# Second layer's ReLU joined with VectorE's weighting, and the scores' two spread products made one

## What is computed

```python
# graph attention, per graph
Wh = h @ W;  f_i = Wh @ a1;  f_j = Wh @ a2
e = leaky_relu(f_i[:, :, None] + f_j[:, None, :], 0.2)
e = where(adj > 0, e, NEG_INF)
out = elu(softmax(e) @ Wh)

# first mixture, per token; top_i, routing_weights from the router
h1 = relu(features @ expert_w1 + expert_b1)
h2 = relu(h1 @ expert_w2 + expert_b2)
expert_out = h2 @ expert_w3 + expert_b3
combined = sum(take(expert_out, top_i) * routing_weights)
```

## Time and profile before

| | before |
|---|---|
| median of 3 runs | 577.62 us (577.44 to 578.25) |
| profiled execution | 582.93 us |
| its span, first to last instruction | 580.9 us |
| PE busy | 544.8 us (94%) |
| DVE busy | 453.2 us (78%) |
| ACT busy | 420.9 us (72%) |
| POOL busy | 229.0 us (39%) |

### The profile page before, as it was taken

How to read it: one execution, slowest core, us unless ns; L and a number is a source line. 1 busy time by engine, 2 the same in 40 slices (tenths; PEclk the granted TensorE clock), 3 DMA queues, 4 the chain that set the end, 5 groups by cost and what they waited for, 6 DMA issues and landing times.

```text
span 580.9 us, 14943 instructions
## 1 busy us (share of the span) xinstructions
PE 544.8 (94%) x3713; PEld 450.9 (78%) x3745; DVE 453.2 (78%) x1679; ACT 420.9 (72%) x1113; POOL 229.0 (39%) x442
## 2 busy tenths in 40 slices
PE   7789899999999999999999999999977999999993
PEld 6556677778787777878777787767756999999993
DVE  3776879889898898988989888776567187777777
ACT  1356577878878788787887878877653578888883
POOL 5212214442344424344243342431322046666665
PEclk9999999999999999999999999999997599999997
DMA  7604405043150422504225051131220567777732
GB/s 162 163 29 136 138 28 164 23 143 107 59 163 6 157 94 70 163 1 163 72 91 162 2 163 52 60 110 30 81 74 3 172 206 241 236 219 219 224 117 72
DMA packets 79135, 66.45 MB, mean 114 GB/s; under 512 B 10218, under 2 KB 64762, under 8 KB 79098
## 3 DMA queue, kind: packets, MB, share of 16 engines
q1 hardware_dynamic: 67914, 61.39, 34.9%
q10 hardware_dynamic: 11184, 4.63, 2.9%
HBM read 61.58 MB, written 4.42 MB: 114 GB/s over the span
## 4 chain that ended last, share of the span: by engine, by line
PE 72%; DVE 9%; issue 7%; ACT 5%; POOL 2%; DMA 2%; ACTq 0%; DVEq 0%; SPq 0%; POOLq 0%
PE bank L1593 12%; PE bank L1580 11%; PE bank L1893 5%; PE wide L206 5%; PE wide L1893 5%; PE bank L1903 5%; PE wide L1903 4%; PE bank L1572 3%; PE bank L1574 2%; PE wide L239 2%; PE bank L1573 2%; PE wide L231 2%; PE wide L199 2%; ACT h L851 2%; PE bank L1546 2%
## 5 line engine op out<-in xcount | busy, mean ns | idle before, releaser
L1593 PE MATMUL bank<-w,h2w 128*128 128x128 f32 x768 | 104.4, 279 | 6.5 <-DVE h2w L1147 6.5
L1593 PEld LDWEIGHTS bank<-w,h2w 128*128 128x128 f32 x768 | 94.8, 192 | 12.6 <-DVE h2w L1147 10.0
L1580 PE MATMUL bank<-h,w 128*128 128x512 f32 x192 | 100.1, 603 | 1.0 <-ACT h L851 1.0
L846 ACT ACTIVATE h<-bank,b 128x512 f32<-128x512 f32 x96 | 66.2, 689 | 37.9 <-PE bank L1580 37.7
L851 ACT ACTIVATE h<-bank,b 128x512 f32<-128x512 f32 x96 | 66.3, 691 | 13.2 <-PE bank L1574 12.7
L1147 DVE TENSOR_TENSOR h2w<-h,wide_w 128x512 f32<-128x512 f32 x96 | 64.9, 676 | 9.4 <-ACT h L846 8.5
L1572 PE MATMUL bank<-xnTh,w1h 128*128 128x512 f32 x96 | 61.9, 645 | 0.0
L100 POOL TENSOR_TENSOR route_var_eps<-route_mean_var,eps 128x4 f32<-128x4 f32 x17 | 11.2, 660 | 115.6 <-DVE route_mean_var L93 115.6
L100 POOL TENSOR_TENSOR at_var_eps<-at_mean_var,eps 128x4 f32<-128x4 f32 x32 | 12.2, 381 | 95.9 <-DVE at_mean_var L93 95.9
L268 ACT ACTIVATE at_pr<-at_lk,at_nm 128x128 f32<-128x128 f32 x124 | 39.9, 412 | 2.4 <-DVE at_nm L303 1.7
L1574 PE MATMUL bank<-xnTl,w1h 128*128 128x512 f32 x96 | 38.0, 396 | 0.0
(11 more groups left out here) (312 smaller groups left out, 1373.3 us busy)
## 6 DMA issues: line engine op xcount, KB each, us to landing
wide_w<-w_scratch SPq DMA_DIRECT2D x96, 256.0 KB, 4.7
mask<-in_L_ffn_W SPq DMA_DIRECT2D x124, 128.0 KB, 2.4
x<-in_x SPq DMA_DIRECT2D x16, 256.0 KB, 5.6
adj_in<-in_adj SPq DMA_DIRECT2D x16, 256.0 KB, 6.2
wide_w<-bmix_scratch SPq DMA_DIRECT2D x16, 256.0 KB, 3.6
xin<-in_x SPq DMA_DIRECT2D x15, 256.0 KB, 6.0
out<-at_pr ACTq DMA_DIRECT2D x8, 256.0 KB, 3.0
out<-at_prT ACTq DMA_DIRECT2D x7, 256.0 KB, 2.8
```

The costliest lines, as they stand in the source:

```text
L846: a.activation(h2[:, e % 2, :], b_h2[:, :], ACT.Relu, bias=b2[:, e:e + 1]).then_inc(h2_ready, 1)
L1580: pe.matmul(b_h2[:, :], w2[:, e, :], h1[:, e % 2, :], start=True, stop=True).then_inc(l2_done, 1)
L1593: last = pe.matmul(b_out[:, s], h2w[:, e % 2, s], w3[:, e, :], start=False, stop=(e == E0 - 1), skip_group_check=True)
```

## The change

**Experts.** `relu2` is gone from ACT. `weigh` reads layer 2's PSUM bank itself and takes max(z, -b2) times the weight. What this lacks against relu(z + b2), the weight times b2, is put into the third bias: POOL lays b2 out (`second_bias`), PE multiplies it by w3 in six products, DVE adds that to b3 (`merge_biases`), all once, before the experts start. `layer2` now waits for the `weigh` before it, and expert 1 of each round uses the bank `b_pool`. `weigh` 3, 4 and 5 stand earlier in DVE's list, and `route_exp` earlier in ACT's.

**Scores.** The order of `src` changes, so that each graph's six rows lie in partitions of their own (32 to a graph). ACT forms `rows` with a scale and a bias from SBUF columns (`inhalf`, `three`), and in four more instructions of 32 partitions the diagonal blocks of a new tile `blocks`; PE makes one product of the two instead of `spread`'s five.

```diff
+def form_rows(st, a, turned, inhalf, three):
+
+    a.activation(st["rows"][:, :], turned[:, :], ACT.Identity, bias=three[:, 1:2], scale=inhalf[:, 0:1])
+    for t in range(GG):
+        q = slice(t * P // GG, (t + 1) * P // GG)
+        last = a.activation(st["blocks"][q, t * P:(t + 1) * P], turned[q, :], ACT.Identity, bias=three[q, 0:1],
+                            scale=inhalf[q, 1:2])
+    last.then_inc(st["rows_ready"], 1)
+
-    a.activation(st["rows"][:, :], st["bank"].bitcast(BF16)[:, 0:P], ACT.Copy).then_inc(st["rows_ready"], 1)
+    form_rows(st, a, st["bank"].bitcast(BF16)[:, 0:P], inhalf, three)
...
     pe.matmul(st["bank"][:, :], identb[:, :], mask[:, cols(g)], start=True, stop=False, skip_group_check=True)
-    pe.matmul(st["bank"][:, :], st["rows"][:, :], spread[:, 0, :, :].rearrange("p t d -> p (t d)"), start=False,
-              stop=False, skip_group_check=True)
-    for t in range(GG):
-        last = pe.matmul(st["bank"][:, t * P:(t + 1) * P], spread[:, 1, t, :], st["rows"][:, :], start=False,
-                         stop=True, skip_group_check=True)
-    last.then_inc(st["z_done"], 1)
+    pe.matmul(st["bank"][:, :], st["rows"][:, :], st["blocks"][:, :], start=False, stop=True, skip_group_check=True)\
+        .then_inc(st["z_done"], 1)
...
-            def relu2(n, e):
-                a.wait_ge(l2_done, n + 1)
-                need(a, h2w_ready, n - 1)
-                a.activation(h2[:, e % 2, :], b_h2[:, :], ACT.Relu, bias=b2[:, e:e + 1]).then_inc(h2_ready, 1)
...
-                v.wait_ge(h2_ready, n + 1)
+                v.wait_ge(l2_done, n + 1)
                 v.wait_ge(w_loaded[e], 16 * g + 16)
                 need(v, l3_done, n - 1)
-                v.tensor_tensor(h2w[:, e % 2, :], h2[:, e % 2, :], wide_w[:, e, :], ALU.mult).then_inc(h2w_ready, 1)
+                v.scalar_tensor_tensor(h2w[:, e % 2, :], h2_bank(e), b2neg[:, e:e + 1], wide_w[:, e, :], ALU.max,
+                                       ALU.mult).then_inc(h2w_ready, 1)
...
                 pe.wait_ge(h1_ready, n + 1)
-                need(pe, h2_ready, n)
-                pe.matmul(b_h2[:, :], w2[:, e, :], h1[:, e % 2, :], start=True, stop=True).then_inc(l2_done, 1)
+                if e != 1:
+                    need(pe, h2w_ready, n - 1 if e == 2 else n)
+                pe.matmul(h2_bank(e), w2[:, e, :], h1[:, e % 2, :], start=True, stop=True).then_inc(l2_done, 1)
```

More of the change, by code:

```diff
@@ L154, in attn_stage @@
     st["rows"] = sb("rows", P, BF16)
+    st["blocks"] = sb("blocks", GW, BF16)
     st["lk"] = sb("lk")
@@ L400, in build @@
     centre = sb("centre", [P, P])
-    spread = sb("spread", [P, 2, GG, P], BF16)
+    inhalf = sb("inhalf", [P, 2])
+    three = sb("three", [P, 2])
+    halfmark = sb("halfmark", [P, 2, GG, 16])
+    threemark = sb("threemark", [P, 2, GG, 3])
+    unread = sb("unread", [P, 2 * P], BF16)
     zero = sb("zero", [P, GG, 2])
@@ L731, in _ @@
             p.memset(at1["src"][:, :], 0.0).then_inc(spread_step, 1)
[L732 to L738, removed]
+            p.memset(at0["blocks"][:, :], 0.0).then_inc(spread_step, 1)
+            p.memset(at1["blocks"][:, :], 0.0).then_inc(spread_step, 1)
+            p.memset(unread[:, :], 1.0).then_inc(spread_step, 1)
+            p.memset(halfmark[:, :, :, :], 0.0).then_inc(spread_step, 1)
+            p.memset(threemark[:, :, :, :], 0.0).then_inc(spread_step, 1)
+            p.wait_ge(spread_step, 7)
+            for mark, width in ((halfmark, 16), (threemark, 3)):
+                p.affine_select(out=mark[:, :, :, :], in_=mark[:, :, :, :], compare_op=ALU.not_equal, fill=1.0, base=0,
+                                pattern=[[-16, 2], [-32, GG], [-1, width]], channel_multiplier=1)\
+                    .then_inc(spread_step, 1)
             def later_constants():
@@ L874, in late_attention @@
                 a.wait_ge(at0["rows_done"], N + 1)
-                a.activation(at0["rows"][:, :], b_out.bitcast(BF16)[:, 0:P], ACT.Copy).then_inc(at0["rows_ready"], 1)
+                form_rows(at0, a, b_out.bitcast(BF16)[:, 0:P], inhalf, three)
                 for q in range(2):
@@ L971, in body @@
                     attn_act_prT(at0, a, i + 2)
-                if run and i0 > 0:
-                    relu2(n + 3, 3)
-                    relu1(n + 4, 4)
                 if route and i0 != -LEAD["route"]:
                     route_exp()
+                if run and i0 > 0:
+                    relu1(n + 4, 4)
                 if attn1:
-                    attn_act_rows(at1, a, i - 1)
+                    attn_act_rows(at1, a, inhalf, three, i - 1)
                 if route:
@@ L1347, in body @@
                     route_first(i + 1)
[L1348 to L1349 removed]
+                if run:
+                    weigh(n + 3, i, 3)
                 if route:
@@ L1355, in body @@
                     attn_dve_y(at0, v, i + 2)
-                if run and i0 > 0:
-                    weigh(n + 3, i, 3)
+                if run:
+                    weigh(n + 4, i, 4)
                 if route and i0 != -LEAD["route"]:
@@ L1659, in late_attention @@
                               start=True, stop=False, skip_group_check=True)
-                    pe.matmul(late_z[q], at0["rows"][:, :], spread[:, 0, 2 * q:2 * q + 2, :].rearrange("p t d -> p (t d)"),
-                              start=False, stop=False, skip_group_check=True)
-                    for t in range(2):
-                        last_t = pe.matmul(late_z[q][:, t * P:(t + 1) * P], spread[:, 1, 2 * q + t, :], at0["rows"][:, :],
-                                           start=False, stop=True, skip_group_check=True)
+                    last_t = pe.matmul(late_z[q], at0["rows"][:, :], at0["blocks"][:, lane[q]], start=False, stop=True,
+                                       skip_group_check=True)
                     last_t.then_inc(at0["z_done"], 1)
@@ L1732, in body @@
                     if i0 == -LEAD["attn0"]:
-                        pe.wait_ge(spread_step, 6)
-                    busy_fill(i0, 12 if i0 == -LEAD["attn0"] else 28)
+                        pe.wait_ge(spread_step, 9)
+                    busy_fill(i0, 12)
                     if i0 == -LEAD["route"]:
+                        pe.wait_ge(b2_step, E0 + 2)
+                        for e in range(E0):
+                            mixed_bias = pe.matmul(b_out[0:KB, 0:P], b2cols[:, e, 0:KB], w3[:, e, :], start=(e == 0),
+                                                   stop=(e == E0 - 1))
+                        mixed_bias.then_inc(b2_step, 1)
+                        busy(b_pool, 6)
                         route_transpose(i, i0)
@@ L1751, in body @@
                     pe.wait_ge(mask_ready, i + 3)
-                    attn_pe_scores(at0, pe, identb, mask, spread, i + 2)
+                    attn_pe_scores(at0, pe, identb, mask, i + 2)
                 if run and i0 > 0:
@@ L1806, in body @@
                 if attn1:
-                    attn_pe_scores(at1, pe, identb, mask, spread, i - 1)
+                    attn_pe_scores(at1, pe, identb, mask, i - 1)
                 if run:
```

75 lines of the change are left out of this document (43 added, 32 removed).

## The result

| | before | after |
|---|---|---|
| median (lowest to highest, 6 runs each) | 577.93 us (575.06 to 580.82) | 607.14 us (603.79 to 609.12) |
| profiled execution | 582.93 us | 603.79 us |
| its span | 580.9 us | 602.0 us |

The ratio is 1.050 (95% interval 1.047 to 1.053). The kernel became slower, as predicted, but by 29.2 us where I had said 17.5: the time is above the range's upper end of 602.

What follows compares the result with a forecast made beforehand. The bound was taken to be PE's issue plus half a microsecond of waits a round. Terms of +13.9, +1.2, -2.2 and +4.6 made +17.5 us, so 595.1 us against the median of 577.62; range 584 to 602.

Steps and rivals of the forecast that it cites:

- R: Time from first start to last end of ACT's five instructions ahead of the mask: 2.24 us, no overlap where partitions change.
- The hand-over: Time from the end of ACT's `rows` work until PE starts on it: 0.06 us, taken from the late attention.
- First half: First attention, rounds 1 to 13: new stall of 1.27 us before the mask's product, net +1.07 a round, +13.9 in all.
- Second half: Second attention: PE waits 0.78 us for expert 5's `relu1`, the gain of 0.68 is eaten; +0.10 a round, +1.2 over 12.
- Round 1: Has the first attention's full stall, but pools nothing and keeps its second-half gain of 0.68 us: +0.4 in all.
- Rounds 14 to 16: Have no first attention and keep an estimated gain of 0.5 us each; with round 1's 0.68, -2.2 in all.
- (c): DVE becomes PE's gate, PSUM's bank held until a `weigh` of 1.2 us rather than 0.75 is done: 601.6 us, chance 0.07.
- The start: Up to the first `xe`: +2.8 us, from the first `rows` and round -1's (+1.1); bias work beside waiting engines.
- Late attention: Nothing covers `rows` there, so the longer chain is waited for: +1.8 us.
- (a): ACT's instructions overlap across partitions after all: R of 1.94, 8.4 us less, 586.7 us, chance 0.22.
- (b): The blocks are cheap: R of 1.0, -11.7 us, 565.9 us, faster than before; sign turns at R of 1.6; chance 0.11.
- (d): `layer3` of expert 3 still waits 0.48 us, its `weigh` queued behind another wait: 595 us again, no chance of its own.

Runs made afterwards that it cites:

- e3: The changed kernel with the second bias laid out by POOL one round earlier; 604.73 us, ratio 1.044 to the kernel before.
- e8: As e7, and in round 0 the `weigh` of expert 3 stands ahead of the mask and the router's first steps; 571.28 us, ratio 0.988.
- e4: The changed kernel with each of the four blocks formed on all 128 partitions (full width), so start partitions no longer change; 592.44 us, ratio 1.024.
- two blocks: The changed kernel with only the blocks of graphs 0 and 1 formed, of four; 581.73 us, ratio 1.007 to the kernel before.
- e7: The kernel before with the experts' part of the change alone, and the second bias laid out by POOL one round earlier; 572.87 us, ratio 0.992.
- e5: The changed kernel with only the first of the four diagonal blocks formed (one block); 574.18 us, ratio 0.994 to the kernel before.

## Why the prediction was right in sign and too small

The increase came out 11.7 us above the forecast (29.2 for 17.5). The profiled pair shows 3.6 of this (a span of 602.0 for 598.4): 5.2 in the start, 1.8 in rounds 2 to 13 and 2.6 in rounds 14 and 15, less 1.2 in round 1 and 4.8 from there to the end. The other 8.3 is how far the two profiled executions lie from their medians. The mechanism, ACT's chain R ahead of the mask and in ACT's queue, held. The step that failed is the start, where the bias work was put at nothing; it costs 4.2 us in the trace, of which the times of `e3` bear out 2.4.

- **What bounds the kernel.** Right. PE's starts decide; freed of the scores' part, PE fills its full rounds without a gap (`e8`).
- **R.** Right: 2.18 for 2.24, from the rule that nothing overlaps at a change of start partition. `e4` confirms the reason: without that change the pace falls to 0.34, and with one block it is 0.34 on 32 partitions too.
- **The hand-over.** Mis-sized. I took 0.06 from the late attention; in this full round it is 0.24 (282.28 to 282.52, and the same with two blocks and with full width). By the single instructions it goes by the place in the program: 0.25 for the first attention in the rounds of the loop (3 to 12), 0.15 for it in the rounds written out and in the start, 0.06 for the second attention where it waits (422.02) and for the late one (457.11 to 457.17). Why is open. Against my 0.06 this is some 2.2 us in all.
- **First half.** The stall, counted from the end of the cover (279.76 and 1.36, 281.12), is 1.40 where I said 1.27: 0.18 more of hand-over, 0.06 less of R.
- **Second half.** Right in place and size: the wait moved to `layer2` of expert 5: 0.62 by the row, and 0.78 by starts (297.50 to 298.39, less the 0.11 that this step takes in `e8`), for 0.78 predicted. The gain of 0.68 was eaten, as said. A full round is 25.80 for 25.7, and 12 of them cost 15.8 for 14.0.
- **Round 1.** I gave its first half the full stall; it became 0.77 shorter than before instead of 0.4 longer. The stall is there (1.03 at 77.43). The parts alone say where: with the scores' part round 1 grows by 0.89, which is what I had for it (1.27 less 0.40), and with the experts' part it shrinks by 1.69, where I had 0.48. Why it gains so much more there is open.
- **Rounds 14 to 16.** Wrong in sign. I let them keep 0.5 each, because they have no first attention. Rounds 14 and 15 lost 0.94 and 0.64, while with the experts' part alone they change by +0.04 and -0.75. So it is the scores' part again: the trace after has, in round 14, the mask waiting 0.24 for `blocks` at 422.02, `p_xn` late by 0.29 at 423.81, and `layer3` waiting 0.85 for `weigh` at 411.99 (0.64 before). I had not walked ACT's queue there. The rest of the loss is not traced.
- **Weighting.** 0.74 for 0.75, and no `layer2` of a full round waits for it: rival (c) is out there. But it did occur once, in round 0, where I had looked at no row.
- **The start.** The step that failed: +7.96 for +2.8. "The bias work lies beside waiting engines" took POOL as idle without placing the work in its queue. It stands behind `route_rstd`, which waits for VectorE, and PE waits for it. PE's starts, and then the first `xe`, against the kernel before:

| | fillers | router's transposes | first `layer2` | first `xe` |
|---|---|---|---|---|
| changed kernel | +0.3 | +4.5 | +5.6 | +8.0 |
| with early bias (`e3`) | +1.7 | +1.8 | +2.9 | +6.3 |
| scores' part alone | +0.2 | +0.3 | +1.4 | +4.0 |
| experts' part, early bias (`e7`) | -0.6 | -0.6 | -0.5 | +1.9 |

The bias work, put at nothing, is 4.2: 2.31 of waiting, and then products and fillers at the lower clock. The `rows` of round -1 are 1.1, as said. Round 0, also put at nothing, is 2.4, and as much in `e7`, without the scores' part; the 0.87 that the moved `weigh` takes off its wait is the only piece of it that is shown, since the scores' part alone has 2.6 there too, in a trace with 3.4 us at a granted clock of 0.50. The first `rows`, +1.7 as said, are +1.7 in `e3` and +0.3 in the changed kernel, because there PE's first transpose starts at 12.83, and at 14.26 before and in `e3`. That isn't the change: `e7` and `e8`, alike up to there, have 12.78 and 14.25. So in this trace luck hid 1.4 us of the miss. Between the columns of the table the granted clock was 1.00 but for one stretch of 3.4 us each: in the changed kernel from 30.0, in the bias products, in `e3` from 66.1 and with the scores' part alone from 63.9.
- **Late attention.** Right: the wait ahead of its mask is 2.06 for 0.15, the mask comes 1.90 later behind the last `xe`, for 1.8 predicted.
- **The clock and the two profiled executions.** The stretch to the end is 3.5 shorter after, though its mask is 1.9 late. Windows of both kernels in the second mixture (columns as above, the granted clock third from the end):

```profile
450.00:461.00 11.00, 11.00 (x47) 9.79 (x48) 1.60 (x8) 5.47 (x16) 0.00 (x0) 0.50 0.48 143
```
```profile
477.20:596.00 118.80, 115.45 (x1027) 114.52 (x1025) 85.22 (x353) 93.54 (x318) 66.94 (x90) 1.00 0.67 202
```

The mixture starts at 449.99 before and 475.99 after. Before, it ran at 1.2 GHz up to 462.0; after, only up to 477.1. From its start to the end, before takes 4.9 us longer (130.9 for 126.0). Without that the pair differs by 26.0. The medians differ by 29.2, because the profiled execution of before was 5.0 above its median and that of after 3.3 below. The 4.9 of the clock is of the size of the first of these, but the other executions have no trace to show that it is the same; why the others of after are 3.3 slower than the one with a trace is open.

Of the rivals, (a) and (b) are out by R = 2.18, (c) holds in round 0 alone, and (d) did not occur. That (b) would have been faster than before is not borne out: at R = 1.0 a line between one block (574.18) and two (581.73) gives 577.5, no change, where I said 565.9 and put the point of no change at R = 1.6. The first `xe` of the kernels with one and two blocks comes 4.2 and 5.7 later than before, where (b) had 0.9 for start and late attention together. At R = 1.0 the same line through their full rounds gives 23.72 where (b) has 23.63, since the wait begins at R near 0.8. The rest is in how the executions spread: by the profiled spans (567.4, 577.2 and 580.9) the line gives 9.2 us less than before, against my 11.7, but the execution with one block that has a trace is 5.1 below its median, and that of before 5.0 above.

## What to carry to other kernels

When work moves between engines, walk the queue of the engine that receives it up to the next thing that the bound engine needs; the same scores' part cost 2.5 us a round with six ReLUs in ACT's queue and 1.8 (25.80 less 23.98) without them. A chain of short dependent instructions is priced by its first start to last end. One-off work in a start-up needs its place in the queue too, for there nothing hides it. And two edits that share a queue should be timed apart: here one was worth keeping, and the pair hid it.

## What the runs showed of the hardware

- ACT instructions on 32 partitions at changing start partitions follow each other at 0.46 us, the same ones on all 128 partitions at 0.34. Less data was slower. On 32 partitions with the start partition unchanged it is 0.34 too (`e5`).
- An ACT instruction of 128 columns from PSUM with scale and bias columns takes 0.43 to 0.48, whether on 32 or 128 partitions.
- PE's mask product, standing for ACT, started 0.25 us after the end of ACT's last instruction in the loop's rounds, in all five kernels that wait there, 0.15 in rounds written out, and 0.06 in the late attention.
- The granted clock was 0.50 for 6.8 to 24 us in or after the late attention in every trace, and in most also for some stretches of 3.4 us in the start, at places that differ from one kernel's trace to the next.
